# Two ways to drop the zero halves from k and q times the random features, in a one-core graph kernel

## The reference, cut to what matters

```python
def softmax_kernel(data, proj, is_query):            # data (b, h, n, 64), proj (256, 64)
    data_dash = einsum('bhnd,md->bhnm', data * 64 ** -0.25, proj)
    diag = sum(data * data, -1, keepdims=True) * 0.5 * 64 ** -0.5
    if is_query:
        m = max(data_dash, axis=-1, keepdims=True)
    else:
        m = max(data_dash, axis=(-3, -2, -1), keepdims=True)   # one number for all of k
    return 256 ** -0.5 * (exp(data_dash - diag - m) + 1e-4)
qkv = (x @ w_qkv.T)...                               # q, k, v by head
q_prime, k_prime = softmax_kernel(q, proj_mat, True), softmax_kernel(k, proj_mat, False)
out = (q_prime @ (k_prime.T @ v)) / (q_prime @ sum(k_prime))   # by head, then @ w_proj.T + b_proj
```

## Time and profile before

| | us |
|---|---|
| median of 3 runs | 1719.46 (1717.51 to 1719.79) |
| the profiled execution, its own time | 1719.8 |
| its span | 1719.8 |
| TensorE busy | 1582.3 (92%) |
| VectorE busy | 1137.4 (66%) |
| ScalarE busy | 680.8 (40%) |
| mean granted TensorE clock | 0.971 of 2.4 GHz |

### The profile page before, as it was taken

How to read it: one execution, slowest core, us unless ns; L and a number is a source line. 1 busy time by engine, 2 the same in 40 slices (tenths; PEclk the granted TensorE clock), 3 DMA queues, 4 the chain that set the end, 5 groups by cost and what they waited for, 6 DMA issues and landing times.

```text
span 1719.8 us, 25185 instructions
## 1 busy us (share of the span) xinstructions
PE 1582.3 (92%) x9743; PEld 1199.8 (70%) x9809; DVE 1137.4 (66%) x2618; ACT 680.8 (40%) x1359; POOL 409.8 (24%) x251
## 2 busy tenths in 40 slices
PE   3989999999989889999999999998999999986987
PEld 2556666555655568888888888888888976666664
DVE  6678664104565999999987697668765833785223
ACT  3420001122232466777667764346534621441110
POOL 3788888888300000000000000000000000002331
PEclk9989999999999999999999999999999999996999
DMA  9335535454652413224320254335413224545941
GB/s 358 82 59 119 113 79 124 62 92 74 191 183 87 143 46 114 87 91 127 109 70 28 83 172 167 102 118 191 139 39 95 85 71 153 212 180 208 317 151 50
DMA packets 194889, 213.67 MB, mean 124 GB/s; under 512 B 81359, under 2 KB 149597, under 8 KB 194770
## 3 DMA queue, kind: packets, MB, share of 16 engines
q1 hardware_dynamic: 118146, 187.01, 33.0%
q0 software_dynamic: 75760, 22.70, 8.3%
q10 hardware_dynamic: 864, 2.36, 0.4%
HBM read 144.74 MB, written 68.40 MB: 124 GB/s over the span
## 4 chain that ended last, share of the span: by engine, by line
PE 72%; DVE 18%; ACT 3%; issue 3%; DMA 3%; SPq 0%; POOLq 0%; POOL 0%; ACTq 0%; DVEq 0%
PE bank L1075 18%; PE bank L905 13%; PE bank L906 13%; PE bank L904 12%; DVE junk L1480 4%; PE bank L1245 4%; PE bank L1233 3%; PE bank L1129 2%; DVE eb L1515 2%; DVE eb L1524 2%; PE bank L1101 1%; PE bank L1144 1%; PE bank L1006 1%; PE bank L1114 1%; PE bank L914 1%
## 5 line engine op out<-in xcount | busy, mean ns | idle before, releaser
L1075 PE MATMUL bank<-hb,eb 128*128 128x193 f32 (+3 forms) x2400 | 417.4, 331 | 13.3 <-ACT node L1922 7.1
L1075 PEld LDWEIGHTS bank<-hb,eb 128*128 128x128 f32 (+3 forms) x2400 | 400.2, 190 | 23.8 <-issue 10.2
L2119 POOL DMA_INDIRECT table<-amount,place x170 | 344.6, 2027 | 70.1 <-issue 49.1
L2125 POOL IOTA iota8i<- 128x8 int32 x1 | 0.1, 140 | 957.0 <-DMA node_rows<-node 957.0
L1515 DVE SCALAR_TENSOR_TENSOR eb<-shift_b,as_low,shift_b 128x640 f32<-128x640 f32 (+1 forms) x240 | 196.3, 860 | 0.3 <-PE bank L1075 0.2
L1908 ACT ACTIVATE eb<-eb,asd 128x640 f32<-128x640 f32 (+1 forms) x240 | 181.3, 811 | 28.7 <-DVE eb L1515 28.7
L1480 DVE CUSTOM_DVE_ANT_0 junk<-ab,absent 128x1250 bf16<-128x1250 f32 x120 | 174.3, 1452 | 1.6
L1524 DVE SCALAR_TENSOR_TENSOR eb<-eb,count 128x1280 f32<-128x1280 f32 (+1 forms) x120 | 174.4, 1453 | 0.2 <-ACT eb L1908 0.2
L904 PE MATMUL bank<-w_o_hi,aT_hi 128*128 128x384 bf16 (+1 forms) x360 | 119.2, 331 | 0.0
L904 PE MATMUL bank<-wg_hi,x1T_hi 128*128 128x384 bf16 (+3 forms) x360 | 119.0, 331 | 0.1
L905 PE MATMUL bank<-w_o_lo,aT_hi 128*128 128x384 bf16 (+1 forms) x360 | 118.9, 330 | 0.0
(11 more groups left out here) (290 smaller groups left out, 2967.7 us busy)
## 6 DMA issues: line engine op xcount, KB each, us to landing
w<-in_w SPq DMA_DIRECT2D x16, 1152.0 KB, 13.1
shift_b<-shift_rows SPq DMA_DIRECT2D x24, 625.0 KB, 5.8
h_rows<-h_row SPq DMA_DIRECT2D x27, 388.0 KB
hb<-h_rows SPq DMA_DIRECT2D x12, 873.0 KB
ar<-node_rows SPq DMA_DIRECT2D x27, 384.0 KB, 3.2
table<-zero POOLq DMA_DIRECT2D x3, 3054.0 KB, 19.1
tab<-table SPq DMA_DIRECT2D x27, 312.5 KB, 3.4
qk_rows<-qk_row SPq DMA_DIRECT2D x12, 625.0 KB
```

Of the source, the lines that this page charges most:

```text
L1075: ins = T.matmul(bank[w // 2][0:M, c0:c0 + GC + 1], p[0:K, u, w * P:w * P + M], hv[0:K, t, 0:GC + 1], start=opens and u == 0 and w % 2 == ...
L2119: G.indirect_dma_start(tables[i], bass.IndirectOffsetOnAxis(place[:, c:c + 1], axis=0), amount16[:, c:c + 1], None, compute_op=ALU.add).th ...
```

## The change

`feats` becomes 128 by 256: the projection in partitions 0 to 63 and again in 64 to 127, with no zeros.

For the mix, `pair_in` loads k and q by head: partitions 0 to 63 hold the high parts of a head and 64 to 127 the low parts, the two heads behind each other. So `dash` is, for each head, two matmuls of 256 columns with contraction over 128: (high; low) by the high features, and by the low ones. That is four matmuls of 256 columns for three of 512, and it adds the product low by low, which was left out. Each load is two transfers of 64 partitions where it was one of 128.

For the greatest k, `qk_out` stays as it is, and `k_top` takes two row tiles at once (30 of it): 12 matmuls of 256 columns with contraction over 64, head 0 from partitions 0 to 63 into bank 4, head 1 from partitions 64 to 127 into bank 5, by turns. VectorE takes the greatest of 128 by 1024 over both banks (for the last tile, of 98 rows, on its own). A `k_top` now waits until the one before it is read (`k_max`, i).

```diff
             if n % 2 and 2 * c + part:
-                for t in range(4 * c + 2 * part - 2, 4 * c + 2 * part):
-                    yield "k_top", NT * (n // 2) + t
+                yield "k_top", HALF * (n // 2) + 2 * c + part - 1
...
-        feats = [put(f"feats_{p}", [128, 2 * FEATS], BF16) for p in ("hi", "lo")]
+        feats = [put(f"feats_{p}", [128, FEATS], BF16) for p in ("hi", "lo")]
...
             def k_top(i):
-                pair, t = divmod(i, NT)
+                pair, b = divmod(i, HALF)
                 pe.wait_ge("feats_lo", 1)
                 pe.wait_ge("qk_lo", NC * (2 * pair + 1))
-                pe.wait_ge("k_max", i - 1)
-                dash_into(4 + i % 2, qk_out[0], t).then_inc(sem["top_mm"], 1)
+                pe.wait_ge("k_max", i)
+                for u in range(2):
+                    t = 2 * b + u
+                    for n, (k_part, f_part) in enumerate(((0, 0), (0, 1), (1, 0))):
+                        for hh in range(2):
+                            hs = slice(hh * HD, (hh + 1) * HD)
+                            ins = T.matmul(bank[4 + hh][0:rows(t), u * FEATS:(u + 1) * FEATS], qk_out[0][hs, k_part, at(t)],
+                                           feats[f_part][hs, :], start=n == 0, stop=n == 2)
+                ins.then_inc(sem["top_mm"], 1)
...
             def dash(pair, kind, t):
...
-                pe.wait_ge(f"{kind}_in{pair % 2}", 16 * (pair // 2 + 1))
+                pe.wait_ge(f"{kind}_in{pair % 2}", 32 * (pair // 2 + 1))
                 pe.wait_ge("mix_exp", g - 1)
-                dash_into(3 + g % 2, (keys_of if kind == "k" else queries_of)(pair), t).then_inc(sem["dash_mm"], 1)
+                parts = (keys_of if kind == "k" else queries_of)(pair)
+                for hh in range(2):
+                    for f in range(2):
+                        ins = T.matmul(bank[3 + g % 2][0:R, hh * FEATS:(hh + 1) * FEATS], parts[:, hh, at(t)],
+                                       feats[f][:, :], start=hh == 0 and f == 0, stop=f == 1, skip_group_check=True)
+                ins.then_inc(sem["dash_mm"], 1)
...
             def k_top(i):                                  # VectorE
-                R = rows(i % NT)
+                t0 = 2 * (i % HALF)
+                dashes = banks[:, 4 * 512:6 * 512].rearrange("p (h u m) -> p h u m", h=2, u=2)
                 ve.wait_ge("top_mm", i + 1)
-                V.tensor_reduce(kmax[0:R, i:i + 1], bank[4 + i % 2][0:R, :], AX.X, ALU.max).then_inc(sem["k_max"], 1)
+                for ta, tb, R in alike(t0, t0 + 2):
+                    ins = V.tensor_reduce(kmax[0:R, 2 * i + ta - t0:2 * i + ta - t0 + 1],
+                                          dashes[0:R, :, ta - t0:tb - t0, :], AX.XYZ, ALU.max)
+                ins.then_inc(sem["k_max"], 1)
...
-                S.dma_start(keys_of(pair)[:, :, :], qk_rows[1, pair]).then_inc(sem[f"k_in{i}"], 16)
+                for s in range(2):
+                    S.dma_start(keys_of(pair)[s * HD:(s + 1) * HD, :, :],
+                                qk_rows[1, pair][:, s, :].rearrange("(h d) n -> d h n", h=2)).then_inc(sem[f"k_in{i}"], 16)
```

More of the change, by code:

```diff
@@ L553, in program @@
         sem.update({name: sem[first] for name, (first, _) in TAKEN_OVER.items()})
-        bank = [ctx.enter_context(nc.psum_tensor(f"bank{i}", [128, 512], F32)) for i in range(8)]
+        banks = ctx.enter_context(nc.psum_tensor("bank", [128, 8 * 512], F32))
+        bank = [banks[:, 512 * i:512 * (i + 1)] for i in range(8)]
         def dram(name, shape, dt=F32):
@@ L591, in program @@
         diag, k_shift = put("diag", [P, 2, NT, HEADS]), put("k_shift", [P, NT, HEADS])
-        feats = [put(f"feats_{p}", [128, 2 * FEATS], BF16) for p in ("hi", "lo")]
+        feats = [put(f"feats_{p}", [128, FEATS], BF16) for p in ("hi", "lo")]
         m_col, eps = put("m_col", [P, LH, NT]), put("eps", [P, 1])
         ident16 = put("ident16", [128, 128], BF16)
-        over = cursor[0]
+        over = cursor[0] = max(cursor[0], r_spent + 2 * size([128, KF, CAP], F32))
         count = put("count", [P, NT, N], U16)
@@ L717, in program @@
         kmax, top = put("kmax", [P, PAIRS * NT]), put("top", [128, 4])
-        pf = put("pf", [128, 2 * FEATS])
-        r_e = max(after, cursor[0])
+        pf = put("pf", [128, FEATS])
+        r_e = max(after, cursor[0] + size([128, FEATS], F32))
         cursor[0] = r_d
@@ L1008, in norms @@
                 ins.then_inc(sem["norm_mm"], 1)
-            def dash_into(b, parts, t):
-                R = rows(t)
-                return three(bank[b][0:R, :], [parts[:, p, at(t)] for p in range(2)], [f[:, :] for f in feats],
-                             True, True)
             def k_top(i):
-                pair, t = divmod(i, NT)
+                pair, b = divmod(i, HALF)
                 pe.wait_ge("feats_lo", 1)
                 pe.wait_ge("qk_lo", NC * (2 * pair + 1))
-                pe.wait_ge("k_max", i - 1)
-                dash_into(4 + i % 2, qk_out[0], t).then_inc(sem["top_mm"], 1)
+                pe.wait_ge("k_max", i)
[7 more added lines that the diff above has]
+                ins.then_inc(sem["top_mm"], 1)
             def top_turn(_):
@@ L1082, in dash @@
                 g = dash_of(pair, kind, t)
+                R = rows(t)
                 if g == 0:
-                    pe.wait_ge("k_max", PAIRS * NT)
+                    pe.wait_ge("k_max", PAIRS * HALF)
                     pe.wait_ge("diag_in", 2 * PAIRS * NC)
-                pe.wait_ge(f"{kind}_in{pair % 2}", 16 * (pair // 2 + 1))
+                pe.wait_ge(f"{kind}_in{pair % 2}", 32 * (pair // 2 + 1))
                 pe.wait_ge("mix_exp", g - 1)
-                dash_into(3 + g % 2, (keys_of if kind == "k" else queries_of)(pair), t).then_inc(sem["dash_mm"], 1)
+                parts = (keys_of if kind == "k" else queries_of)(pair)
[4 more added lines that the diff above has]
+                ins.then_inc(sem["dash_mm"], 1)
             def k_sum(pair, t):
@@ L2298, in pair_in @@
                     sy.wait_ge("dash_mm", dash_of(pair - 2, "q", NT - 1) + 1)
-                S.dma_start(queries_of(pair)[:, :, :], qk_rows[0, pair]).then_inc(sem[f"q_in{i}"], 16)
+                for s in range(2):
+                    S.dma_start(queries_of(pair)[s * HD:(s + 1) * HD, :, :],
+                                qk_rows[0, pair][:, s, :].rearrange("(h d) n -> d h n", h=2)).then_inc(sem[f"q_in{i}"], 16)
             def divide(pair, b):
```

15 lines of the change are left out of this document (7 added, 8 removed).

## The result

Changed kernel: median 1713.02 us of 11 runs (1706.52 to 1717.79) against 1719.79 for the kernel before, timed beside it (1717.51 to 1724.53, 11 runs). The ratio is 0.9963, 95% interval 0.9951 to 0.9975: 6.4 us less, with 4.3 to 8.4 as its bounds. The forecast was 1705.5, 14.3 us less. It lies inside the predicted range, but the change is under half of the forecast.

What follows compares the result with a forecast made beforehand. TensorE alone bounds k and q of the first three pairs; in the mix VectorE is as full until 840 us, then TensorE leads. `dash` 10 plus greatest k 4 off 1719.8, median 0.3 lower: 1705.5; range 1695 to 1719.

Steps and rivals of the forecast that it cites:

- a stall of 0.5 us, once a pair: Greatest k: TensorE waits where the `qk` part between steps lasts 0.87 us and a reduction with hand-over 1.4.
- 0.8 us more, in three such loops: Greatest k, pairs four and five beside the counts: the chain's loop goes from 2.85 to 3.64 us, -2.4 us in all.
- a piece of chance: Clock in the 81 us from 464: some 10 us at the lower level, up to 5 us lost, outside the sum.
- The greatest k, TensorE: `k_top`: 12 matmuls two at a time in 0.67 us plus 0.1 per shape change, a step 0.87 us for 1.29.
- The greatest k, the wait: `k_top` waits for the whole last reduction, 1.22 to 1.34 us, where half sufficed; greatest k still gains 4 us together.
- The mix: `dash`: Mix: four matmuls of 256 save 25.4 us of TensorE; a third of 39.6 us on the chain is 13.2, taken as 10.
- The loads: `pair_in`: two more transfers for k and q each, hidden, cost nothing; without cover some 5 us for each of five pairs.
- Tables: First count: tables there at about 457.6 us, count at 465.3, so up to 7.7 us may be won ahead; 4.9 fit.
- 4: Rival: contraction over 64 saves nothing in `k_top`, matmuls one behind the other, 1.51 us a step; 1720; chance 0.13.
- 5: Rival: `k_top` matmuls one behind the other and drained at each change, 1.83 us a step; 1727.5; chance 0.10.
- 3: Rival: `k_top` two at a time, each change drains the pipeline (0.26 us), 1.19 us a step; 1712; chance 0.12.
- 2: Rival: VectorE takes over in the mix, only the stretch behind 840 pays, 5 us instead of 10; 1710; chance 0.11.

Runs made afterwards that it cites:

- e9: Changed kernel plus 47 useless filling matmuls where its trace shows TensorE idle between first count and first `dash`: 1705.86 us, ratio 0.9928.
- e13: e9 plus 37 more filling matmuls at TensorE's idles in the mix: 1702.32 us, ratio 0.9916.
- e12: Kernel before plus 26 filling matmuls at its own TensorE idles between first count and first `dash`: 1715.59 us against 1717.04, ratio 0.9987.
- e1: Kernel before with only the new `dash` and its loads, greatest k as before from a second copy of the features with zeros: 1713.14 us, ratio 0.9967.
- e4: Changed kernel with `k_top`'s products of head 0 ahead of those of head 1, in each tile three and three: 1713.38 us, ratio 0.9969.
- e2: Kernel before with only the new `k_top`, the mix with the old `dash`: 1719.15 us, ratio 1.0001.
- e3: Kernel before with only the changed kernel's whole wait, each two `k_top` waiting until both of the last two are read: 1723.02 us, ratio 1.0020.
- e5: Changed kernel with all of head 0 first, then head 1, each waiting only for its own bank's reduction: 1709.80 us, ratio 0.9936.
- e10: e5 plus 35 filling matmuls where its own trace shows TensorE idle: 1712.74 us, ratio 0.9956.
- e6: Changed kernel with two matmuls a `dash` instead of four, low features' products left out, result not the reference's: 1710.40 us, ratio 0.9924.

## Why the prediction was wrong

**The step that failed** is the sum's treatment of waits: "a stall of 0.5 us, once a pair" and "0.8 us more, in three such loops" price an idle at its length, and the clock stood outside the sum as "a piece of chance", at nothing, though the same sentence says that "more idle TensorE may bring more of it". The change made idles of 2.4 us out of 1.2 and 1.0, at 486 and 533 us, one of 2.0 out of 1.5 at 574, and a new one of 1.7 at 471; those of 2.5 and 2.3 at 495 and 516 stayed. Each of the six had 3 to 7 us of half clock behind it, where the kernel before has two such (at 497 and 518 us). It is no fixed price: in e9 an idle of 2.3 us at 494 us was left, and the clock stayed at 1.00.

Between first count and first `dash` 24 us more passed at the lower clock. The filled kernels give the exchange rate: e9 against the changed kernel 8.8 us for 34 us of half clock, e13 against e9 6.9 for 27, e12 against before 3.2 for 10: 0.25 to 0.31 us of time for each us, from single executions. At that rate the change's 24 us there cost some 6.4 us, and its 13 us more in the mix 3.6: 10 us that the forecast lacked.

The times of all executions bear both out. With the half-clock time of an execution taken as 2 x (1 - mean clock) x time, the 34 executions of the kernel before that were timed beside e1 to e4 differ by 0.35 us of time for each us of it, the 11 of the changed kernel by 0.22, and the 209 executions of all kernels here, each against the mean of its own, by 0.30. The mean clock is 0.964 in the changed kernel and 0.973 in those 34: 31 us more of half clock, an estimate of 9 us at 0.30. That alone would be a correlation; that the clock carries the time, the fillers show. A clue had been read and not used: the prediction's own estimate of 10 us at the lower level in 81 us, in a stretch where TensorE idles for 2.7, 2.4 and 1.2 us.

**The greatest k, TensorE: right.** Two at a time, 0.1 us a change, 0.85 us for 0.87 forecast. The first three pairs won 4.0 us in e2 for 4.9 forecast.

**The greatest k, the wait: right in kind, wrong in size.** TensorE does wait for the whole reduction (1.22 us in the mean, as forecast), 8.5 us in sum between count and `dash` where the kernel before waits 4.9. Forecast for `k_top` was -4, measured 0 (e2). The wait alone costs 3.4 us (e3); cut by head, 3.3 us of waits are left and the kernel is 1709.8 (e5). With the clock held the forecast's 4 is 4.3 (e12 to e9).

**The mix: `dash`, right in mechanism, its size cut by the clock.** Forecast -10. It measured -7.8 us by the stage (-7.2 in e1) and 0.33% by time, 5.7 us (e1). With the clock held on both sides it is 13.2 (e12 to e13), which is what the chain's third had said; part of that is e13's 7 us less of half clock, some 2 us, which leaves 11. So without the clock the sum was, if anything, a little low: 14 us for some 15 (11 here and 4.3 for the greatest k).

**The loads: right.** Nowhere waited for.

**Tables: the slack was mis-sized.** "Up to 7.7 us may be won" took one execution's last scatter; in the others with all scatters it lies 1 to 7 us later.

**Rivals.** None of the five was it. 4 and 5 fall with the pairs at 0.11 us. 3 falls with 0.1 us a change. 3 (1712) and 2 (1710) are nearest to the measured 1713 in number, by luck: 3's mechanism isn't there. 2's premise, TensorE idling more in the mix, is true; but the mix went from 396.5 to 389.6 us with fillers (e13), so VectorE was not all that held it at 395. That the measured time lies inside the range is luck as well: the range was wide for rivals that weren't it, and the clock was no term of it.

Not settled: why e10 does not gain, why one idle of over 2 us brings the lower clock and another (e9, 494 us) doesn't, how much of e6's saving returns in time (2.6 or 6.7 us), and what in the tail behind the mix (51 to 63 us of half clock in kernels alike there) is chance.

## To carry to other kernels

When work is taken from TensorE, read the granted clock of each stretch before and after, and price a new idle (those with the lower clock behind them were 1.5 to 2.7 us long here) at its length plus the slower work behind it; here a us at the lower level cost about 0.3 us of time. Where a trace shows such idles, useless matmuls in them, as many as fit and nowhere else, can be worth a try: 84 of them in a kernel of this size brought 0.47% on top of the change's 0.37%. It isn't sure to work (e10), and what counts is the time and the mean clock over several executions, since one stretch of one kernel varied by over 6 us between executions. And when a finer hand-over is merged into one, ask what the waiting engine does afterwards, not only how long it waits.

## What the runs showed of the hardware beyond that

- The two row halves of TensorE took their matmuls each in its own order: with three of head 0 ahead of three of head 1 the first and the fourth start together (e4: a pair every 0.11 us, 0.77 us from the first start to the next `qk`, 0.76 in the changed kernel). The Trainium skill (TensorE: Matmul & The Clock Gate, Part 3) calls matmuls strictly first in, first out in start and end; between halves this trace shows otherwise for the starts (its ends are modelled), and the measurement decides. An interleaved order isn't needed, which is what makes the wait by head (e5) possible.
- A change between contraction 128 and row tiles of 64 cost 0.1 us each way (0.31 us to the next start where 0.216 is the pace, 0.21 where 0.11 is).
- TensorE with less to do can be busy nearly as long as before: 26 us of work fewer, 5.7 us of busy time fewer (e6, one execution).
